# Dispatching the second choice's rows ahead of the experts, and adding both result arrays at the end

## The reference

```
t = _to_tokens(x)                          # 8192 tokens of 128 numbers
gate_logits = _ln_t(t) @ Wg + bg           # 8 experts
top_w, top_i = top_k(gate_logits, 2);  top_w = softmax(top_w)
for e in range(8):
    h = gelu(xf @ W1[e] + b1[e])           # 128 -> 512
    out = out + w_dense[:, e] * (h @ W2[e] + b2[e])   # 512 -> 128
t = t + out
```

## Time and profile before

| | us |
|---|---|
| median of 3 runs | 1159.59 (1155.31 to 1161.32) |
| the profiled execution | 1150.0 |
| its span, first to last instruction | 1148.2 |
| first row load of the experts | 673.9 |
| last result sent by POOL | 1115.2 |

### The profile page before, as it was taken

How to read it: one execution, slowest core, us unless ns; L and a number is a source line. 1 busy time by engine, 2 the same in 40 slices (tenths; PEclk the granted TensorE clock), 3 DMA queues, 4 the chain that set the end, 5 groups by cost and what they waited for, 6 DMA issues and landing times.

```text
span 1148.2 us, 24693 instructions
## 1 busy us (share of the span) xinstructions
PE 710.1 (62%) x7641; PEld 541.2 (47%) x7642; DVE 758.4 (66%) x2465; ACT 615.8 (54%) x1531; POOL 445.3 (39%) x492
## 2 busy tenths in 40 slices
PE   0036888888888888739500025757675777797760
PEld 0003666666666666625300014545554565676650
DVE  4795899999999999975484004334443455686653
ACT  0024898898888889816412014434443465576550
POOL 3001243434334343310058763555554643454350
PEclk9996899999999999958755556877787788898885
DMA  9735999900000000000001121211121213432219
GB/s 203 173 73 153 165 26 167 18 0 0 0 0 0 0 0 0 0 1 0 1 33 39 53 83 38 57 54 56 56 58 51 65 54 85 108 92 76 77 57 276
DMA packets 102861, 70.39 MB, mean 61 GB/s; under 512 B 52645, under 2 KB 93158, under 8 KB 99752
## 3 DMA queue, kind: packets, MB, share of 16 engines
q1 hardware_dynamic: 92392, 42.65, 24.5%
q0 software_dynamic: 9152, 18.89, 5.0%
q10 hardware_dynamic: 1280, 8.39, 3.2%
HBM read 36.04 MB, written 33.61 MB: 61 GB/s over the span
## 4 chain that ended last, share of the span: by engine, by line
PE 35%; DVE 26%; issue 26%; ACT 4%; DMA 4%; another core or an unknown queue 1%; POOL 1%; SPq 1%; DVEq 0%; ACTq 0%; POOLq 0%
PE PT L1330 11%; DVE L L919 6%; DVE pl L909 4%; PE S L1314 3%; PE S L1316 3%; PE S L1315 3%; PE PT L1322 2%; DMA xt<-in_x 2%; DVE rowstat L442 2%; DVE xt L944 2%; DMA shared<-expert_out 2%; PE S L1148 1%; PE A L1171 1%; PE PT L1196 1%
## 5 line engine op out<-in xcount | busy, mean ns | idle before, releaser
L630 POOL DMA_INDIRECT expert_out<-yo,rows_all x156 | 158.8, 1018 | 200.8 <-ACT yo L809 162.3
L801 ACT ACTIVATE hf<-S,b_sb,inv_hscale 128x256 f32<-128x256 f32 x312 | 153.7, 567 | 72.8 <-remote 42.8
L624 POOL DMA_INDIRECT routed<-pay,pos x128 | 132.3, 1034 | 121.4 <-DVE pay L1059 81.1
L712 ACT ACTIVATE L<-L,lmin 128x128 f32<-128x128 f32 x512 | 159.2, 390 | 0.4
L919 DVE CUSTOM_DVE_ANT_0 L<-S,biasN,logit_scale 128x128 f32<-128x128 f32 x512 | 148.4, 345 | 2.5 <-issue 1.9
L1105 DVE TENSOR_SCALAR hh<-hf,hscale 128x512 f16<-128x512 f32 x156 | 77.5, 497 | 87.9 <-ACT hf L801 64.5
L607 POOL TENSOR_TENSOR og<-gt,on 128x256 f32<-128x256 f32 x64 | 46.5, 727 | 229.3 <-DVE on L932 229.3
L1107 DVE SCALAR_TENSOR_TENSOR hl<-hf,hscale,hh 128x512 f16<-128x512 f32 x156 | 117.4, 753 | 5.6
L792 ACT ACTIVATE fx_h<-A 128x256 f16<-128x256 f32 x39 | 14.9, 383 | 183.3 <-PE A L1304 68.4
L1330 PE MATMUL PT<-w_h,hh 128*128 x624 | 91.6, 229 | 16.3 <-issue 10.7
L1304 PE MATMUL A<-identity,rows_all 128*128 128x128 f32 x78 | 18.3, 323 | 134.4 <-DMA rows_all<-routed 72.3
(11 more groups left out here) (235 smaller groups left out, 2085.7 us busy)
## 6 DMA issues: line engine op xcount, KB each, us to landing
rows_all<-routed SPq DMA_DIRECT2D x78, 132.0 KB
routed<-blank SPq DMA_DIRECT2D x2, 5031.0 KB, 41.6
shared<-expert_out SPq DMA_DIRECT2D x16, 512.0 KB, 11.4
xt<-in_x SPq DMA_DIRECT2D x8, 512.0 KB, 24.6
shared<-in_L_conv_ln_w ACTq DMA_DIRECT2D x8, 512.0 KB, 11.8
shared<-in_L_conv_ln_b ACTq DMA_DIRECT2D x8, 512.0 KB, 10.4
out<-xt SPq DMA_DIRECT2D x8, 512.0 KB, 9.7
expert_out<-yo,rows_all POOLq DMA_INDIRECT x156
```

What stands on the lines that cost most here:

```text
L624: pool.indirect_dma_start(routed[k], bass.IndirectOffsetOnAxis(ap=pos[k][:, i:i + 1], axis=0), pay[:, i, :], None).then_inc(scattered[k], 16)
L630: pool.indirect_dma_start(expert_out[t // SLOT_TILES], bass.IndirectOffsetOnAxis(ap=row_place[t % IN_BUFS][:, k, W + 1:W + 2], axis=0), yo ...
L712: last = nc.scalar.activation(L[p][:, h, i, :], L[p][:, h, i, :], ACT.Exp, scale=-1.0, bias=lmin[p][:, h * R + i:h * R + i + 1])
L801: last = nc.scalar.activation(hf[p][:, b, :], S[2 * p + pair][:, k * TILE:(k + 1) * TILE], ACT.Gelu, scale=inv_hscale[:, 0:1], bias=b1_fla ...
```

## The change

POOL now scatters all 64 groups of choice 1 right behind those of choice 0, and only then begins to send results; `LEAD` and `due` are gone. SP waits for both choices' scatters before it loads the first tile. Nothing is loaded or added inside the expert loops any more (`extra`, `add_first`, `y0_in`, `y0_added` are gone). In the tail SP loads both arrays: `expert_out[0]` into `shared` as before, and `expert_out[1]` into `pay`, whose rows are 132 numbers apart, so each 512-byte row is a piece of its own. DVE adds first the one, then the other.

```diff
-            LATER = SLOT_TILES + IN_BUFS
             sp.wait_ge(scattered[0], 16 * HALF)
-            for t in range(SLOT_TILES):
+            sp.wait_ge(scattered[1], 16 * HALF)
+            for t in range(TILES):
                 load_rows(t)
-            sp.wait_ge(scattered[1], 16 * HALF)
-            for t in range(SLOT_TILES, LATER):
-                load_rows(t)
-
-            sent_through(SLOT_TILES - 1)
-            for c in range(CH):
-                if c:
-                    for t in range(LATER + BODY * (c - 1), LATER + BODY * c):
-                        load_rows(t)
-                for f in range(2):
-                    sp.dma_start(shared[f * C:(f + 1) * C, chunk(c), :], outputs_v[0][f, :, chunk(c), :]).then_inc(y0_in, 16)
-            for t in range(LATER + BODY * (CH - 1), TILES):
-                load_rows(t)
 
             sent_through(TILES - 1)
-            sp.wait_ge(y0_added, HALF // R)
             for c in range(CH):
                 for f in range(2):
-                    sp.dma_start(shared[f * C:(f + 1) * C, chunk(c), :], outputs_v[1][f, :, chunk(c), :]).then_inc(y_in[c], 16)
+                    for back, out_v in ((shared, outputs_v[0]), (pay, outputs_v[1])):
+                        sp.dma_start(back[f * C:(f + 1) * C, chunk(c), 0:W], out_v[f, :, chunk(c), :]).then_inc(y_in[c], 16)
...
             pool.wait_ge(meta_ready, 2)
-            due = [LEAD + (HALF - LEAD) * t // (SLOT_TILES - 8) for t in range(SLOT_TILES)]
-            for t in range(SLOT_TILES):
-                for i in range(due[t - 1] if t else 0, min(HALF, due[t])):
-                    scatter_rows(1, i)
-                send_rows(t)
-            for t in range(SLOT_TILES, TILES):
+            for i in range(HALF):
+                scatter_rows(1, i)
+            for t in range(TILES):
                 send_rows(t)
...
-            tile_steps(dve, tile_step, add_first)
-
-            dve.wait_ge(y0_added, HALF // R)
+            tile_steps(dve, tile_step)
+
             for c in range(CH):
-                dve.wait_ge(y_in[c], 32)
-                nc.vector.scalar_tensor_tensor(xt[:, chunk(c), :], shared[:, chunk(c), :], y_scale[:, 0:1], xt[:, chunk(c), :],
+                k = chunk(c)
+                dve.wait_ge(y_in[c], 64)
+                chain.link(nc.vector.scalar_tensor_tensor(xt[:, k, :], shared[:, k, :], y_scale[:, 0:1], xt[:, k, :],
+                                                          ALU.mult, ALU.add))
+                nc.vector.scalar_tensor_tensor(xt[:, k, :], pay[:, k, 0:W], y_scale[:, 0:1], xt[:, k, :],
                                                ALU.mult, ALU.add).then_inc(y_added, 1)
```

More of the change, by code:

```diff
@@ L338, in build @@
         y_sent = [sem(f"y_sent{b}") for b in range(YO_BUFS)]
-        y0_in = sem("y0_in")
-        y0_added = sem("y0_added")
         y_in = [sem(f"y_in{c}") for c in range(CH)]
@@ L348, in build @@
         outv = out[0].rearrange("c (f i) j -> f c i j", f=2)
-        LEAD = 8
         def chunk(c):
@@ L384, in build, with tile_steps @@
         LOOPS = (5, 45, 77)
-        def tile_steps(engine, step, extra=None, experts=None):
+        def tile_steps(engine, step, experts=None):
             assert LOOPS[2] == TILES - 1 and all((b - a) % BODY == 0 for a, b in zip(LOOPS, LOOPS[1:]))
@@ L398, in tile_steps @@
                         step(BODY * g + LOOPS[n] + k, (LOOPS[n] + k) % BODY, es[k:k + 2])
-                        if n == 1 and extra and k % 2:
-                            extra(g, k // 2)
             for s in range(LOOPS[2], TILES + 2):
@@ L1110, in _ @@
             dve.wait_ge(table_ready, 2)
-            def add_first(g, j):
-                if j == 0:
-                    dve.wait_ge(y0_in, 32 * g + 32)
-                k = bass.ds(g * CR + j * R, R)
-                nc.vector.scalar_tensor_tensor(xt[:, k, :], shared[:, k, :], y_scale[:, 0:1], xt[:, k, :],
-                                               ALU.mult, ALU.add).then_inc(y0_added, 1)
-            tile_steps(dve, tile_step, add_first)
-            dve.wait_ge(y0_added, HALF // R)
-            for c in range(CH):
-                dve.wait_ge(y_in[c], 32)
-                nc.vector.scalar_tensor_tensor(xt[:, chunk(c), :], shared[:, chunk(c), :], y_scale[:, 0:1], xt[:, chunk(c), :],
+            tile_steps(dve, tile_step)
+            for c in range(CH):
+                k = chunk(c)
[3 more added lines that the diff above has]
+                nc.vector.scalar_tensor_tensor(xt[:, k, :], pay[:, k, 0:W], y_scale[:, 0:1], xt[:, k, :],
                                                ALU.mult, ALU.add).then_inc(y_added, 1)
```

## The result

The changed kernel takes 1176.39 us (median of 4, 1173.48 to 1177.15), the kernel before 1158.34 (median of 4, 1155.31 to 1161.32): ratio 1.0151, 95% interval 1.0118 to 1.0185, 18.05 us slower, a small difference but clear of the noise. Forecast were 1178.7, in the range 1165 to 1198, plus 19.1 us. Profiled were executions of 1175.76 us (span 1174.0) and 1150.0 (span 1148.2).

What follows compares the result with a forecast made beforehand. POOL's indirect DMA bursts were taken to bound the experts' first half, PE the second. 82.3 - 6.7 - 72.8 - 1.7 + 17.5 + 0.5 = plus 19.1 us on the median 1159.6 gave 1178.7, range 1165 to 1198.

Steps and rivals of the forecast that it cites:

- The lead: Ahead of the experts: 64 scatters of choice 1 delay every expert step by 82.3 us, bounds 81 and 85.
- first loop: Five expert passes, 250.8 us before: with sends alone each takes 35.6 us, together 178.0, minus 72.8 us.
- written-out steps: Steps from 676.3 to 715.5 us, 39.2 us before: two ACT stalls shrink or go, minus 6.7 us.
- the first tile's stall: ACT's 6.83 us wait in the first tile's gelu, in the written-out steps: 4 of 6.8 us taken as saved.
- The rival in which the stalls are not the scatters': First loop and written-out steps stay slow for another reason: plus 98.6 us, 1258 in all; chance 0.05.
- bursts of indirect DMAs on POOL: First half of the expert stage: these hold the tiles, with ACT standing 5.69 us in one pair.
- Moved at the same price: Scatters go from beside the experts to ahead of them at equal cost: last tile's end moves plus 1.1 us.
- The tail's second array: Loading expert_out[1] into pay in 512-byte pieces in the tail: plus 17.5 us, bounds 10.7 and 22.3.
- rival of the cheap tail: Tail loads all run at 393 GB/s, tail grows 2.6 us: plus 4.2 in all, 1163.8; chance 0.07.
- The end: Last chunk's additions and store start, nearly covered by the first three chunks' stores: plus 0.5 us, bounds 0 and 2.
- The pass starts: PE's idle gap of 6.3 to 7.9 us at each of nine pass starts, 61 us in all, expected to stay.
- the faster rival: PE's gap at pass starts shrinks with emptier DMA queues; at 3 us the kernel takes 1145; chance 0.04.

Runs made afterwards that it cites:

- chip Q: A chip without stalls: the kernel before, repeated word for word, took 1068.63 us there; the changed kernel, word for word, 1161.28 us, ratio 1.088.
- the loads among the row loads: Kernel before with 31 unread loads of 512 KB put among the row loads of the first four passes: 1162.13 us, ratio 1.003.
- chip S: A chip with stalls, on which the unchanged kernel before took 1159.18 us (median of 29).
- dense version: Changed kernel with the second results array loaded into pay without row padding, in 8 KB pieces: 1156.37 us, 4.9 under the changed kernel.

## Why the prediction was right, and where it was not

**The lead** was sized exactly (82.3, measured 82.4, and 82.3 on chip Q): 64 instructions at a known pitch on an engine that nothing else overlaps.

**The first loop and the written-out steps** came out within 0.7 us, since a pass with sends alone was in the trace of before as a row. Part of that closeness is chance: four passes average 35.1 us, the fourth has 38.3 with a stall of 1.9 left in it. The other part is the first tile's stall, of which I took away 4 of 6.8 us as a middle between two cases: 2.0 us of it are left (ACT at 768.67), near enough by luck. On the first measurement's chip the statement "what leaves with the scatters is the stall" holds: passes from 56.3 to 35.7 us, "remote" from 93.0 to 7.8 + 3.3 = 11.1 us. The rival in which the stalls are not the scatters' is thereby out for that chip.

**The mechanism behind it was put too generally.** "So in the first half the tiles are held by bursts of indirect DMAs on POOL" is true of one chip and not of the kernel: the repeated kernel before has the same bursts and no stall. It takes a condition of the chip or of the occasion as well. What that is stays open. Crowding by plain DMA traffic does not set the length of the stalls (the loads among the row loads); indirect DMAs and other POOL work were not told apart on chip S. The Trainium skill, Runtime: NRT & Kernel Launch, section on instruction fetch mechanics, says that a sequencer fetches its next code by a DMA queue of its own. The profile does show instruction packets, which the prediction had not looked for, and none in the stalls from 784 to 922 us. So a late fetch is not shown, and not excluded for engines whose fetches may be missing from the profile. The price of the change depends on it: plus 18 us (1.5%) where the stalls are, plus 93 us (8.8%) where they are not. "Moved at the same price" held on the first chip by accident of its stalls.

**The tail's second array was mis-sized**: 17.5 us in the sum, 23.4 measured, over the upper bound of 22.3 that came from the blank fill. I had put the value between W2's row and that of `shared`, in the belief that small pieces might be faster than `shared`'s. They were slower, and W2's row should not have been the neighbour. By the queues view its load moved in packets of 2 KB like W1's (1.15 MB in 563 packets); its 512-byte pieces are on the side of DRAM only. The row with small packets was the blank fill, 516 bytes each (1.87 MB in 3619), which gave the upper bound:

```profile
q1 hardware_dynamic: 563, 1.15, 104.7%
...
q1 hardware_dynamic: 3619, 1.87, 123.8%
```

The loads into `pay` have 512-byte packets, and ran at 179 GB/s where the fill had 188. The dense version shows what the packets are worth beside `shared`'s loads, 0.55 us a chunk. It moves its 4.19 MB in (9.78 - 4.68) x 4 = 20.4 us, 206 GB/s. The rival of the cheap tail (393 GB/s) is refuted: 201 GB/s at a DMA share of 1.14. Why loads of results are this slow, even in large pieces, stays open.

**The end** took 1.4 us more instead of 0.5. I had laid all 16 issues beside the transfer at 0.6 us each; in fact SP was held up to 4.8 us at each load of `shared` and could issue the first store only after the last load (1149.68). That looks like the cause but is not. In the dense version SP is not held, its first store is issued at 1118.30, and from the last chunk's first addition to the end it takes 11.4 us as well. What the two share is the end of the stores. The sum had the last chunk's stores begin at about the time when the others end. They did (SP's last issue is at 1168.5), and from there on they had the engines to themselves, at a falling rate:

```profile
1165.00:1170.00 5.00, 0.00 (x0) 0.00 (x0) 2.35 (x1) 0.00 (x0) 0.00 (x0) 0.50 1.06 393
1170.00:1174.00 4.00, 0.00 (x0) 0.00 (x0) 0.00 (x0) 0.00 (x0) 0.00 (x0) 0.50 0.64 166
```

In the kernel before the last chunk's stores were queued while the others still ran, and the last 5.2 us moved 298 GB/s. That this makes the 0.9 us was not tested by itself.

**The total** owes something to chance. By the profiles' own sum I was 6.7 us too low (19.1 against 25.8); by the medians 1.1 too high. That before's profiled execution was unusually quick made up for the undersized tail. The range held either.

**The pass starts** stayed as foreseen: PE idles 6.36, 5.76 and 6.79 us at the first, sixth and last, so the faster rival is out. (The nine gaps before add up to 62.2 us, where the prediction has 61; nothing hangs on it.)

## What to carry to other kernels

Work moved from beside the bound engine to ahead of it costs its full length (here 1.26 us for each scatter), and gives back only what it really cost where it was (0.19 us on average on a quiet chip, next to nothing until POOL is full and 1.2 us from there on). Read the latter from a pass with it and one without, on more than one chip, before calling a stall a property of the kernel. Fill the waits that an engine has anyway (here six more scatters before the first send, minus 8.5 us) rather than opening a stage for them, and size a transfer by a row with both its piece size and its stride. Take the piece size from the packets in the trace, not from the program.

## What the runs showed of the hardware

- One kernel, word for word, takes 1159.2 us on one chip (median of 29, at least 1146.9) and 1068.6 on another (of 10, at most 1069.4). Between the trace of the first measurement and that of the second of these chips, 78.4 of 81.9 us lie in the stage where indirect scatters run beside the experts, with 93 us of "remote" waits in ACT's rows on the one and none on the other.
- Loads of result rows ran at 230 GB/s in 8 KB pieces from one queue, at 250 from two; the 512-byte pieces into padded rows had 179 GB/s for their share of the time, the same data in 8 KB pieces 206. Stores of the same shape reach 408.
- The number of pieces waiting in a queue, not of DMAs or bytes, holds the issuing engine: SP stood up to 4.76 us at each load of `shared` in the changed kernel's tail, where every other load has 512-byte pieces, and at most 0.99 us with the same sixteen loads of the same bytes in 8 KB pieces.
- An indirect DMA of 128 rows costs POOL 1.262 us, one behind the other (0.96 busy and a gap of 0.30; single ones are up to 1.2 busy). Thirty to 32 in a pass of eight tiles fill POOL, and passes go to 37 to 40 us without any stall.
